# Four engine orders of a gated cross-attention kernel, laid out anew

## The chip, the cores and the metric

One NeuronCore of a Trainium2 chip runs the whole program. The metric is the device time of one execution in microseconds (us), the median of three. The core has five engines that this text names by their labels in the profile: PE (TensorE, matrix multiply; PEld is its weight load), DVE (VectorE), ACT (ScalarE), POOL (GpSimd) and SP, which here only issues DMAs.

## What is computed

Four sequences (b = 0 to 3) of 512 tokens with 128 features pass four residual blocks. A context of 77 rows of 96 features goes with each sequence.

```python
# block 1: attention with a kept top 32 of 77, FiLM, long convolution (S4D), FFN
scores = jnp.einsum('bthd,bghd->bhtg', Q, K) / np.sqrt(DH)        # 4 heads
topv, topi = jax.lax.top_k(scores, 32); probs = jax.nn.softmax(topv, -1)
attn_mean = scatter(probs).mean(heads); c_t = attn_mean @ V
x = layernorm(x_text) * (1 + mod_gate * scale_in) + mod_gate * shift_in
y = irfft(rfft(x) * rfft(K_s4d)) + x * D_skip
xt = x_text + y * (1 + mod_gate * scale_out) + mod_gate * shift_out
xt = xt + gelu(layernorm(xt) @ W1 + b1) @ W2 + b2                 # then a layernorm
# block 2: FFN whose two 512x512 maps are butterfly products
# block 3: attention with 16 heads over the same context
# block 4: eight experts, the best two weighted by a softmax
x = x + jnp.tanh(g) * block(_layernorm(x))                        # around each block
```

## The kernel before, in words

The sequence b is the unit of work, and a tile t = 0 to 3 is 128 of its tokens. All work is cut into named steps such as `film_in/2`, where the number after the slash is b and a digit at the end of the name is a tile, a half or a stage. The dictionary `ORDER` writes out, for each of PE, ACT, DVE and POOL, the order in which that engine takes its steps. Each engine runs its list strictly in order and waits on semaphores for what a step needs. So whatever stands behind a waiting step waits too. No planner runs at build time.

The steps of one sequence are, in order of dependence:

- `score0` to `score3`: PE multiplies, DVE finds the top 32 of 77 for four heads by four rounds of MAX8 and MATCH_REPLACE8 (L1144, L1153), ACT takes the exponentials, POOL picks (`pick`, L1538) and weighs them (`weigh`). In round 1 of a score step DVE adds up what POOL picked for the tile before (`weigh(1)`, L1076), so the DVE stands there until that `pick` is done. `attnT` needs all four `weigh`.
- `film_in`, `dft`, then the spectral product in two halves, `mixr` and `mixi` (seven TENSOR_TENSORs each), `idft`, `film_pre`, `film_out`, `film_add`: FiLM and the long convolution.
- `stat1`, `rs1`, `norm1`, `lift1` (statistics on DVE, root on ACT, scaling on DVE or POOL, transpose on PE), `ffn_up0`, `ffn_up1`, `ffn_down`: the FFN. Then `stat2`, `norm2`, `gain` (POOL), `x1` (the residual sum), `stat3`, `norm3`, `lift3`.
- `fold_up0`, `fold_up1`, `fold_down`: the butterfly block. Then `stat4`, `norm4`, `lift4`.
- `q`, `scoreA0` to `scoreA3` (DVE takes the row maxima), `maxT`, `keyA0` to `keyA2`, `mixA0` to `mixA2`, `normA`, `wo`: attention of 16 heads. Then `stat5`, `lift5`.
- `logits`, `top2`, `units0` to `units3`, `gate0`, `gate1` (POOL), `turn0`, `turn1`, `moe_out`: the experts and the store.

Steps that begin with `s_` are set-up, done once: the convolution's kernel (`s_kgen0`, `s_qarg`, `s_parg`, `s_pexp`, `s_coef`, `s_qal`, `s_pc`, `s_qc`, `s_kern0` to `s_kern3`, `s_freq`), the butterflies made dense (`s_ufly`, `s_udense`, `s_dfly`, `s_dhigh`, `s_dlow` on POOL, `s_t1`, `s_wup`, `s_bup`, `s_t2`, `s_wdn` on PE) and centred or masked weights (`s_m0`, `s_vw`, `s_w1`, `s_cw1`, `s_cwup`, `s_moe`, `s_v1`).

Three other things follow from `ORDER`. The eight PSUM banks are dealt out in the order of PE's list (`place_banks`, first freed, first given), and PE waits for the readers of a bank's former tile. ACT loads a function table whenever the next step needs another set (L782); for a step that leads with a function it does so before it waits. And `made()` finds which engine does a norm, an `x1` or a mix, so these can move from one list to another.

```python
for step, b in SCHEDULE["pe"]:        # likewise "act", "dve", "pool"
    ...
need = table_of.get(func, table[0])
if need != table[0]:                  # an ACT_TABLE_LOAD
```

## Time and profile before

| what | us |
|---|---|
| median of three executions | 362.0 (360.42 to 362.31) |
| the profiled execution | 359.27 |
| its span, first to last instruction | 357.4 |
| PE busy | 269.9 |
| DVE busy | 283.1 |
| ACT busy | 217.0 |
| POOL busy | 195.2 |

The span is 1.9 us shorter than the execution's own time, and that execution is 2.7 us below the median. A busy share is an average over stretches with different limits: until about 226 us DVE works through the sixteen score steps, and from about 162 us to the end PE has the most work. Which of the two is late must be read stretch by stretch. PEclk is the TensorE clock that the chip granted, where 1.0 is 2.4 GHz.

### The profile page before, as it was taken

The page shows a single profiled execution, that of the slowest core. Times are in us where ns is not written, and L with a number is a line of the kernel's source. Part 1 is how long each engine was busy: PE and PEld are TensorE (multiplying, and loading weights), DVE is VectorE, ACT ScalarE, POOL GpSimd, SP SyncE. Part 2 cuts the span into 40 slices and gives each one's busy share as a digit, 9 for nine tenths or more (in the row PEclk, how much of TensorE's full clock was granted, in tenths as well). Part 3 has the DMA queues.
Part 4 walks back from the last instruction along what each step waited for, and adds up shares of the span by engine and source line. Part 5 has one row for each costly group of instructions (what it writes and reads, how often), then busy time and mean ns, then how long its engine had stood idle before and what let it go on. Part 6 is the DMA issues. An engine that isn't in the chain of part 4 may idle for free.

```text
span 357.4 us, 6314 instructions
## 1 busy us (share of the span) xinstructions
PE 269.9 (76%) x1858; PEld 176.5 (49%) x1858; DVE 283.1 (79%) x1402; ACT 217.0 (61%) x472; POOL 195.2 (55%) x271
## 2 busy tenths in 40 slices
...
GB/s 245 383 373 49 1 1 0 1 0 4 3 1 3 0 2 2 1 0 0 3 0 3 0 1 2 0 3 0 2 1 3 0 3 0 2 29 2 0 32 60
DMA packets 6713, 10.82 MB, mean 30 GB/s; under 512 B 660, under 2 KB 4884, under 8 KB 6422
## 3 DMA queue, kind: packets, MB, share of 16 engines
...
q8 instruction: 15, 0.25, 0.3%
...
## 4 chain that ended last, share of the span: by engine, by line
PE 43%; DVE 30%; POOL 16%; issue 3%; DMA 3%; ACT 2%; SPq 1%; POOLq 0%; ACTq 0%; DVEq 0%
PE bank L446 40%; DVE R L1153 8%; DVE V L1144 5%; DMA X<-in_x 3%; DVE MT L1047 2%; POOL arena L1428 2%; POOL bt L1428 2%; POOL k0bd L1428 2%; POOL MT L1428 2%; DVE arena L1047 2%; PE bank L468 2%; POOL sel L1538 1%; DVE st L1093 1%; POOL sel L1428 1%; POOL HN L1485 1%
## 5 line engine op out<-in xcount | busy, mean ns | idle before, releaser
L782 ACT ACT_TABLE_LOAD x37 | 47.5, 1283 | 4.3 <-DMA pack_kgen<-in_kgen 3.7
L1153 DVE MATCH_REPLACE8 R<-V,R 128x77 f32<-128x77 f32 x192 | 40.4, 220 | 0.0
L509 PE MATMUL bank<-pack_first,ASUM 128*77 128x128 f32 x16 | 2.9, 314 | 48.7 <-POOL ASUM L1428 48.7
L788 ACT ACTIVATE arena<-bank 128x512 f32<-128x512 f32 (+2 forms) x67 | 34.8, 598 | 8.1 <-PE bank L446 5.3
L446 PE MATMUL bank<-arena,pack_dft 128*128 128x256 f32 x128 | 34.0, 426 | 5.9 <-DVE arena L1047 4.7
L446 PEld LDWEIGHTS bank<-arena,pack_dft 128*128 128x128 f32 x128 | 27.0, 215 | 13.4 <-DVE arena L1047 6.0
L1428 POOL TENSOR_TENSOR pack_bfly<-pack_bfly,bt 128x512 f32<-128x512 f32 x8 | 8.3, 1049 | 44.8 <-DVE pack_bfly L1047 30.2
L788 ACT ACTIVATE E<-bank,negm,rs 128x77 f32<-128x77 f32 x64 | 21.3, 416 | 18.3 <-DVE negm L1052 18.3
L788 ACT ACTIVATE rs<-mv,cst 128x4 f32<-128x4 f32 x28 | 7.9, 295 | 40.3 <-DVE mv L1096 40.2
L1144 DVE MAX8 V<-R 128x8 f32<-128x77 f32 x192 | 31.1, 222 | 0.0
L509 PEld LDWEIGHTS bank<-pack_first,ASUM 128*77 128x77 f32 x16 | 2.2, 170 | 49.8 <-POOL ASUM L1428 49.6
L1117 DVE TENSOR_REDUCE bt<-bank 128x4 f32<-128x308 f32 x64 | 25.4, 467 | 1.0 <-PE bank L446 0.9
L1428 POOL TENSOR_TENSOR XG<-XG,pack_rows 128x512 f32<-128x512 f32 x4 | 5.1, 1268 | 35.4 <-DVE XG L1052 26.1
L1538 POOL TENSOR_SCALAR sel<-R 128x308 f32<-128x308 f32 x16 | 16.0, 1001 | 15.0 <-DVE R L1153 8.3
L1428 POOL TENSOR_TENSOR k0bd<-sel,w 128x308 f32<-128x308 f32 x16 | 13.3, 829 | 16.9 <-DVE w L1051 16.8
L1047 DVE TENSOR_TENSOR X<-bank,X 128x512 f32<-128x512 f32 x12 | 8.1, 685 | 17.3 <-PE bank L446 17.3
L446 PE MATMUL bank<-pack_bfly,arena 32*128 32x512 f32 (+3 forms) x136 | 21.0, 558 | 0.0
L446 PE MATMUL bank<-pack_moe,LO 128*128 128x512 f32 (+1 forms) x64 | 19.6, 429 | 1.4 <-ACT arena L788 0.7
L1047 DVE TENSOR_TENSOR pack_bfly<-bank,pack_bfly 128x256 f32<-128x256 f32 (+1 forms) x20 | 9.1, 470 | 13.3 <-ACT pack_bfly L788 13.3
L788 ACT ACTIVATE LO<-bank 128x512 f32<-128x512 f32 x16 | 9.4, 596 | 13.8 <-PE bank L468 13.7
L1485 POOL TENSOR_SCALAR HN<-X,rs 128x128 f32<-128x128 f32 x24 | 14.2, 607 | 6.6 <-ACT rs L788 6.6
L788 ACT ACTIVATE arena<-MT 128x128 f32<-128x128 f32 x74 | 17.3, 430 | 0.0
(226 smaller groups left out, 809.1 us busy)
## 6 DMA issues: line engine op xcount, KB each, us to landing
...
```

The source lines that it names most:

```text
L446: return nc.tensor.matmul(out, lhsT, rhs, start=start, stop=stop, **kw)
L468: last = nc.tensor.transpose(o[:, P * t:P * t + P], src[:, b, t, :], I)
L509: last = nc.tensor.transpose(o[0:SK, P * t:P * t + P], ASUM[:, b % 2, t, :], I)
L782: nc.scalar.add_instruction(mybir.InstLoadActFuncSet(name=nc.get_next_instruction_name(), act_func_set_id=need, ins=[], outs=[]))
L788: return nc.scalar.activation(out, in_, func, **kw)
L1047: return nc.vector.tensor_tensor(out, x, y, op)
L1117: nc.vector.tensor_reduce(mx1[:, b % 2, tile, r, :], bank(f"sA{tile}_{r}", b)[:, 0:FLAT] .rearrange("p (h k) -> p h k", h=HG), AX.X, ALU.max)\
L1144: nc.vector.max(V8[:, g % 2, h, r, :], src).then_inc(s["topk_step"], 1)
L1153: nc.vector.match_replace(R8[:, g % 2, r % 2, h, :], V8[:, g % 2, h, r, :], src, NEG)\
L1428: return nc.gpsimd.tensor_tensor(out, x, y, op)
L1485: last = nc.gpsimd.tensor_scalar(dst[:, b, t, :], src[:, b, t, :], rs[:, tile, b, t:t + 1], None, ALU.mult)
L1538: chain(nc.gpsimd.tensor_scalar(sel[:, g % 2, :, :], R8[:, g % 2, 1, :, :], -1.0e38, None, ALU.is_le))
```

## The change

Only `ORDER` changes; every step issues the instructions that it issued before. Four steps go to DVE: `x1/0`, `norm3/2`, `norm4/2` and `norm3/3`. Two go to POOL: `x1/1` and `norm3/1`. The halves of the spectral product stay on their engines (`mixr` on DVE but for b = 3, `mixi` on POOL but for b = 3) and change their places. All four lists are in a new order. The banks follow PE's list, and the number of table loads on ACT follows its list: 37 in the old one, 31 in the new one. The diff is cut where a list goes on.

```diff
--- before.py
+++ after.py
 ORDER = {
     "pe": """
-        s_k0 s_m0 score0/0 s_vw score1/0 s_w1 score2/0 score3/0 score0/1 score1/1 attnT/0 vw/0 s_cw1 s_kern0 s_kern1
-        film_in/0 s_kern2 s_kern3 vw/1 score2/1 s_t1 film_pre/0 score3/1 dft/0 s_freq s_wup score0/2 score1/2 s_cwup
-        s_bup idft/0 vw/2 s_t2 lift1/0 ffn_up0/0 attnT/1 score2/2 ffn_up1/0 s_wdn k1/0 ffn_down/0 film_in/1 vw/3
-        film_pre/1 film_out/0 score3/2 dft/1 score0/3 lift3/0 k1/1 fold_up0/0 fold_up1/0 idft/1 fold_down/0 s_moe
-        film_out/1 s_v1 k1/2 lift4/0 score1/3 attnT/2 lift1/1 q/0 ffn_up0/1 ffn_up1/1 scoreA0/0 scoreA1/0 scoreA2/0
-        film_in/2 scoreA3/0 ffn_down/1 dft/2 film_pre/2 maxT/0 keyA0/0 keyA1/0 score2/3 lift3/1 mixA0/0 fold_up0/1
-        idft/2 film_out/2 fold_up1/1 fold_down/1 keyA2/0 lift1/2 score3/3 mixA1/0 mixA2/0 lift4/1 ffn_up0/2
-        ffn_up1/2 ffn_down/2 q/1 normA/0 k1/3 attnT/3 scoreA0/1 film_in/3 scoreA1/1 film_pre/3 scoreA2/1 wo/0
-        scoreA3/1 dft/3 lift5/0 lift3/2 maxT/1 keyA0/1 keyA1/1 fold_up0/2 units0/0 logits/0 units1/0 idft/3
-        fold_up1/2 units2/0 fold_down/2 units3/0 keyA2/1 mixA0/1 mixA1/1 film_out/3 lift4/2 lift1/3 normA/1 mixA2/1
...
+        s_k0 s_m0 score0/0 score1/0 s_t1 s_vw score2/0 score3/0 score0/1 s_kern0 s_kern1 s_kern2 score1/1 s_kern3
+        score2/1 s_freq s_bup attnT/0 vw/0 s_w1 s_wup s_moe film_in/0 score3/1 dft/0 vw/1 s_t2 film_pre/0 vw/2
+        score0/2 k1/0 idft/0 score1/2 s_cwup attnT/1 film_out/0 s_cw1 film_in/1 score2/2 film_pre/1 lift1/0 dft/1
+        ffn_up0/0 ffn_up1/0 ffn_down/0 vw/3 idft/1 film_out/1 score3/2 s_wdn lift3/0 score0/3 k1/1 fold_up0/0
+        fold_up1/0 fold_down/0 lift1/1 score1/3 ffn_up0/1 ffn_up1/1 ffn_down/1 attnT/2 lift4/0 k1/2 film_in/2 q/0
+        s_v1 scoreA0/0 scoreA1/0 scoreA2/0 scoreA3/0 film_pre/2 score2/3 dft/2 maxT/0 lift3/1 keyA0/0 fold_up0/1
+        fold_up1/1 keyA1/0 fold_down/1 idft/2 keyA2/0 mixA0/0 mixA1/0 film_out/2 score3/3 lift4/1 lift1/2 mixA2/0
+        ffn_up0/2 q/1 ffn_up1/2 scoreA0/1 ffn_down/2 scoreA1/1 attnT/3 normA/0 wo/0 film_in/3 film_pre/3 scoreA2/1
+        scoreA3/1 lift5/0 dft/3 units0/0 units1/0 maxT/1 units2/0 lift3/2 keyA0/1 fold_up0/2 fold_up1/2 mixA0/1
+        keyA1/1 k1/3 fold_down/2 idft/3 keyA2/1 mixA1/1 lift4/2 logits/0 film_out/3 q/2 lift1/3 units3/0 mixA2/1
...
     "act": """
-        s_kgen0 s_cols s_qlag s_plag rs0/0 s_trig rs0/1 s_m0 s_pexp score0/0 s_psin0 norm0/0 s_qsin s_psin1 score1/0
-        s_vw s_qexp score2/0 rs0/2 score3/0 score0/1 vw/0 attnT/0 s_cw1 score1/1 s_kern1 s_kern3 vw/1 s_t1
-        film_pre/0 score2/1 dft/0 s_freq s_wup score3/1 rs1/0 score0/2 s_cwup lift1/0 s_t2 score1/2 vw/2 ffn_up0/0
-        attnT/1 ffn_up1/0 score2/2 k1/0 norm0/1 rs2/0 s_wdn film_pre/1 vw/3 rs3/0 dft/1 rs0/3 score3/2 lift3/0
-        fold_up0/0 score0/3 fold_up1/0 k1/1 rs1/1 rs4/0 s_moe lift4/0 lift1/1 k1/2 attnT/2 q/0 score1/3 ffn_up0/1
-        ffn_up1/1 norm0/2 rs2/1 dft/2 film_pre/2 maxT/0 rs3/1 keyA0/0 lift3/1 keyA1/0 norm0/3 score2/3 fold_up0/1
...
+        s_cols s_kgen0 s_qlag s_plag s_pexp rs0/0 s_trig s_m0 s_psin0 s_psin1 s_qsin score0/0 s_t1 score1/0 rs0/1
+        score2/0 s_vw s_qexp score3/0 s_kern1 s_kern3 score0/1 norm0/0 score1/1 attnT/0 score2/1 s_freq vw/0 s_wup
+        rs0/2 s_moe dft/0 norm0/1 s_t2 film_pre/0 score3/1 vw/1 score0/2 attnT/1 score1/2 vw/2 s_cwup k1/0 rs0/3
+        rs1/0 s_cw1 film_pre/1 lift1/0 dft/1 score2/2 ffn_up0/0 ffn_up1/0 rs2/0 vw/3 s_wdn rs3/0 norm0/2 score3/2
+        rs1/1 lift3/0 fold_up0/0 fold_up1/0 k1/1 score0/3 lift1/1 rs4/0 ffn_up0/1 ffn_up1/1 score1/3 attnT/2 k1/2
+        lift4/0 rs2/1 q/0 film_pre/2 rs3/1 dft/2 maxT/0 score2/3 lift3/1 keyA0/0 fold_up0/1 fold_up1/1 keyA1/0 rs4/1
...
     "dve": """
-        s_kgen0 s_consts s_wq stat0/0 s_qarg s_masks s_k0 stat0/1 s_parg0 nmr0/0 s_parg1 score0/0 s_coef s_edge
-        s_pc0 score1/0 s_pc1 s_pc2 s_pc3 score2/0 stat0/2 s_w1 score3/0 score0/1 weigh3/0 s_qc score1/1 s_kern1
-        film_in/0 s_kern3 score2/1 score3/1 mixr/0 score0/2 film_out/0 nmr0/1 film_add/0 s_bup stat1/0 weigh3/1
-        norm1/0 score1/2 score2/2 ffn_down/0 stat2/0 nmr0/2 norm2/0 film_in/1 stat0/3 stat3/0 score3/2 mixr/1
-        score0/3 film_out/1 weigh3/2 film_add/1 fold_down/0 stat1/1 stat4/0 s_v1 norm1/1 score1/3 scoreA0/0
-        scoreA1/0 scoreA2/0 film_in/2 s_misc scoreA3/0 ffn_down/1 stat2/1 norm2/1 maxT/0 x1/1 stat3/1 norm3/1 nmr0/3
-        mixr/2 score2/3 film_out/2 film_add/2 stat1/2 norm1/2 fold_down/1 stat4/1 score3/3 weigh3/3 ffn_down/2
-        normA/0 stat2/2 scoreA0/1 film_in/3 norm2/2 scoreA1/1 scoreA2/1 stat3/2 wo/0 scoreA3/1 maxT/1 mixi/3 stat5/0
-        film_out/3 units0/0 top2/0 film_add/3 units1/0 fold_down/2 units2/0 stat1/3 stat4/2 units3/0 norm1/3 normA/1
-        wo/1 scoreA0/2 scoreA1/2 stat5/1 scoreA2/2 scoreA3/2 units0/1 maxT/2 ffn_down/3 stat2/3 norm2/3 x1/3 stat3/3
-        top2/1 normA/2 fold_down/3 stat4/3 norm4/3 wo/2 units1/1 moe_out/0 stat5/2 units2/1 units3/1 scoreA0/3
-        scoreA1/3 scoreA2/3 scoreA3/3 units0/2 maxT/3 units1/2 units2/2 units3/2 top2/2 normA/3 wo/3 moe_out/1
...
+        s_kgen0 stat0/0 s_qarg s_wq s_edge s_parg0 s_consts s_k0 s_parg1 s_masks nmr0/0 s_coef s_pc0 s_pc1 score0/0
+        score1/0 s_pc2 s_pc3 stat0/1 score2/0 stat0/2 s_qc stat0/3 score3/0 s_kern1 s_kern3 score0/1 weigh3/0
+        score1/1 s_bup nmr0/1 score2/1 film_in/0 s_w1 nmr0/2 score3/1 mixr/0 score0/2 film_out/0 weigh3/1 score1/2
+        film_add/0 stat1/0 film_in/1 norm1/0 score2/2 mixr/1 ffn_down/0 stat2/0 norm2/0 film_out/1 film_add/1 x1/0
+        stat3/0 stat1/1 score3/2 norm1/1 score0/3 fold_down/0 stat4/0 weigh3/2 score1/3 ffn_down/1 stat2/1 film_in/2
+        norm2/1 s_v1 scoreA0/0 scoreA1/0 scoreA2/0 scoreA3/0 nmr0/3 stat3/1 maxT/0 score2/3 mixr/2 fold_down/1
+        stat4/1 film_out/2 film_add/2 stat1/2 norm1/2 score3/3 scoreA0/1 weigh3/3 s_misc normA/0 ffn_down/2
+        scoreA1/1 wo/0 stat2/2 film_in/3 norm2/2 scoreA2/1 stat5/0 stat3/2 scoreA3/1 maxT/1 norm3/2 units0/0
+        units1/0 units2/0 mixi/3 fold_down/2 stat4/2 norm4/2 film_out/3 film_add/3 stat1/3 norm1/3 top2/0 units3/0
+        scoreA0/2 normA/1 scoreA1/2 scoreA2/2 scoreA3/2 maxT/2 ffn_down/3 stat2/3 wo/1 norm2/3 x1/3 stat5/1 stat3/3
+        norm3/3 normA/2 top2/1 fold_down/3 stat4/3 wo/2 norm4/3 stat5/2 units0/1 units1/1 moe_out/0 units2/1
+        scoreA0/3 units3/1 scoreA1/3 scoreA2/3 scoreA3/3 maxT/3 units0/2 units1/2 units2/2 top2/2 units3/2 normA/3
...
     "pool": """
-        s_row s_ufly pick0/0 s_coef weigh0/0 pick1/0 s_qal weigh1/0 pick2/0 s_udense s_film pick3/0 weigh2/0
-        weigh3/0 pick0/1 s_dfly pick1/1 weigh0/1 pick2/1 film_pre/0 mixi/0 weigh1/1 s_dhigh pick3/1 weigh2/1 pick0/2
-        weigh3/1 s_dlow pick1/2 s_rows k1/0 weigh0/2 weigh1/2 x_bias/0 gain/0 x1/0 pick2/2 norm3/0 mixi/1 film_pre/1
-        weigh2/2 pick3/2 s_v1 weigh3/2 pick0/3 norm4/0 x_bias/1 pick1/3 weigh0/3 gain/1 mixi/2 film_pre/2 weigh1/3
-        k1/1 pick2/3 k1/2 x_bias/2 norm4/1 weigh2/3 pick3/3 weigh3/3 x_bias/3 gain/2 x1/2 film_pre/3 norm3/2 mixr/3
-        k1/3 norm4/2 gate0/0 gate1/0 gain/3 norm3/3 gate0/1 gate1/1 gate0/2 gate1/2 gate0/3 gate1/3
+        s_row s_ufly s_coef pick0/0 s_udense weigh0/0 pick1/0 s_qal s_film pick2/0 weigh1/0 s_dfly pick3/0 weigh2/0
+        pick0/1 weigh3/0 pick1/1 weigh0/1 s_dhigh pick2/1 mixi/0 weigh1/1 s_dlow film_pre/0 pick3/1 weigh2/1 pick0/2
+        weigh3/1 s_rows x_bias/0 pick1/2 film_pre/1 weigh0/2 s_v1 mixi/1 pick2/2 gain/0 norm3/0 weigh1/2 x_bias/1
+        k1/0 k1/1 pick3/2 weigh2/2 pick0/3 weigh3/2 norm4/0 gain/1 pick1/3 x1/1 film_pre/2 norm3/1 mixi/2 norm4/1
+        weigh0/3 pick2/3 x_bias/2 weigh1/3 k1/2 weigh2/3 pick3/3 weigh3/3 gain/2 x1/2 film_pre/3 mixr/3 k1/3 gate0/0
+        gate1/0 gain/3 x_bias/3 gate0/1 gate1/1 gate0/2 gate1/2 gate0/3 gate1/3
```

In the parts left out, PE's new list goes on after `keyA0/0` with `fold_up0/1 fold_up1/1 keyA1/0 fold_down/1 idft/2 keyA2/0 mixA0/0 mixA1/0 film_out/2 score3/3 lift4/1 lift1/2`, and much later with `dft/3 units0/0 units1/0 maxT/1 units2/0 lift3/2 keyA0/1 fold_up0/2 fold_up1/2 mixA0/1 keyA1/1 k1/3 fold_down/2 idft/3`. ACT's new list goes on after `lift1/0` with `dft/1 score2/2 ffn_up0/0 ffn_up1/0 rs2/0 vw/3 s_wdn rs3/0 norm0/2 score3/2 rs1/1 lift3/0`.

## Rows read from the trace of the kernel before

**Rows 1.** Page part 1: busy us, share of the span, instructions.

```profile
PE 269.9 (76%) x1858; PEld 176.5 (49%) x1858; DVE 283.1 (79%) x1402; ACT 217.0 (61%) x472; POOL 195.2 (55%) x271
```

**Rows 2.** Windows, each engine's busy us (x instructions), clock granted to PE, DMA.

```profile
29.00:77.50 48.50, 0.00 (x0) 0.00 (x0) 46.74 (x258) 23.17 (x55) 45.12 (x67) 0.53 0.00 1
95.40:110.90 15.50, 14.79 (x96) 11.60 (x95) 15.36 (x82) 3.71 (x8) 11.95 (x12) 0.99 0.00 1
85.70:162.40 76.70, 67.30 (x472) 51.32 (x472) 74.81 (x437) 39.72 (x91) 61.54 (x81) 0.91 0.01 1
162.40:232.20 69.80, 65.26 (x411) 42.65 (x410) 58.94 (x282) 42.97 (x90) 34.01 (x45) 0.98 0.00 1
232.20:288.85 56.65, 54.66 (x374) 35.57 (x373) 40.34 (x137) 40.29 (x67) 20.39 (x22) 1.00 0.00 1
288.85:354.00 65.15, 61.79 (x420) 34.36 (x416) 32.17 (x150) 41.92 (x77) 9.83 (x11) 0.97 0.04 13
```

**Rows 3.** Page part 5, costliest groups: count, busy, mean ns, idle before.

```profile
L782 ACT ACT_TABLE_LOAD x37 | 47.5, 1283 | 4.3 <-DMA pack_kgen<-in_kgen 3.7
...
L509 PE MATMUL bank<-pack_first,ASUM 128*77 128x128 f32 x16 | 2.9, 314 | 48.7 <-POOL ASUM L1428 48.7
```

**Rows 4.** Timeline of ACT, the start: start us, us, line, op, out<-in, [idle before].

```profile
3.65 1.28 ACT L782 ACT_TABLE_LOAD   x1 [3.65 <-DMA pack_kgen<-in_kgen]
...
5.95 1.28 ACT L782 ACT_TABLE_LOAD   x1
```

**Rows 5.** Timeline of DVE, the first score steps.

```profile
18.03 0.87 DVE L1093 BATCH_NORM_STATS2 st<-X 128x6 f32<-128x128 f32 x4 [1.75 <-DMA X<-in_x]
...
24.19 0.68 DVE L1144 MAX8 V<-bank 128x8 f32<-128x77 f32 x4
...
30.28 0.35 DVE L1047 TENSOR_TENSOR MT<-MT,AO 128x128 f32<-128x128 f32 x1
...
40.49 0.45 DVE L1076 TENSOR_REDUCE sm<-sel 128x4 f32<-128x308 f32 x1
```

**Rows 6.** Timeline of POOL, picks and butterflies.

```profile
31.71 1.00 POOL L1538 TENSOR_SCALAR sel<-R 128x308 f32<-128x308 f32 x1
...
33.58 5.04 POOL L1428 TENSOR_TENSOR MT<-MT 128x128 f32<-128x128 f32 x7
...
44.56 0.46 POOL L1428 TENSOR_TENSOR AO<-AO,MT 128x128 f32<-128x128 f32 x1
...
68.21 0.98 POOL L1538 TENSOR_SCALAR sel<-R 128x308 f32<-128x308 f32 x1
...
79.45 0.65 POOL L1428 TENSOR_TENSOR bt<-pack_bfly 128x64 f32<-128x64 f32 x2
...
91.18 0.46 POOL L1428 TENSOR_TENSOR v<-bt 128x128 f32<-128x128 f32 x1
```

**Rows 7.** Timeline of PE, three steps of the stream.

```profile
156.96 5.41 PE L446 MATMUL bank<-arena,pack_dft 128*128 128x256 f32 x16 [3.84 <-DVE arena L1047]
...
232.22 0.60 PE L509 MATMUL bank<-pack_first,ASUM 128*77 128x128 f32 x4
...
254.34 3.72 PE L446 MATMUL bank<-arena,pack_dft 128*128 128x256 f32 x16 [1.22 <-POOL arena L1428]
```

**Rows 8.** Timeline of POOL, a norm of b = 0.

```profile
143.97 2.35 POOL L1485 TENSOR_SCALAR HN<-X,rs 128x128 f32<-128x128 f32 x4
```

**Rows 9.** Timeline of DVE, half a product twice, and a norm.

```profile
149.62 2.19 DVE L1047 TENSOR_TENSOR MT<-arena,pack_film 128x512 f32<-128x512 f32 x2
...
203.08 1.28 DVE L1047 TENSOR_TENSOR MT<-arena,pack_film 128x512 f32<-128x512 f32 x2
...
312.90 0.87 DVE L1051 TENSOR_SCALAR HN<-X,rs 128x128 f32<-128x128 f32 x4 [0.60 <-ACT rs L788]
```

**Rows 10.** Timeline of ACT, a table load between two activations.

```profile
125.85 1.28 ACT L782 ACT_TABLE_LOAD   x1
127.15 1.27 ACT L788 ACTIVATE arena<-bank,b1f 128x512 f32<-128x512 f32 x2
```

26 lines of the change are left out of this document (13 added, 13 removed).

## The prediction, made before the changed kernel was run

> **What bounds the kernel now.** I read three things in turn: the page's busy times, windows over the stretches, and the timelines of the engines around each moved step. The page gives DVE 283 us and PE 270 us of 357 [rows 1]: no engine has slack to speak of, and neither is full. The windows say where each one rules. Between 29 and 77.5 us PE has nothing, at a granted clock of 0.53, near its lower level of 1.2 GHz, while DVE is busy for 46.7 of 48.5 us [rows 2]. The groups name PE's wait: 48.7 us for POOL's sum of the attention weights, which releases attnT/0 [rows 3]. After film_in/0 leaves PE at 85.7 us, PE is busy for 67.3 of 76.7, 65.3 of 69.8, 54.7 of 56.7 and 61.8 of 65.2 us [rows 2]. Added up, that is 249.0 us of work and 19.3 us of idle time, and PE's last matmul ends at 85.7 + 249.0 + 19.3 = 354.0. DVE is busy for 74.8 of 76.7 us until 162.4 and 58.9 of 69.8 after it [rows 2]. So DVE decides how fast the first half comes and PE how fast the rest goes. I make the sum on PE: the time at which film_in/0 leaves it, its work after that, and its idle time after that.
>
> **PE's work after film_in/0.** Eight steps are now ahead of it that were behind: s_kern2, s_kern3, s_freq, s_wup, s_bup, s_t1, s_moe and score2/1. s_cw1 goes the other way. s_freq, s_wup and s_bup fill most of the window from 95.4 to 110.9, with 14.8 us of PE work [rows 2], less two score steps and s_cwup, some 2.2 us, which gives 12.6. The other five are about 4.1 us and s_cw1 is 1.8. Sum: 12.6 + 4.1 - 1.8 = 14.9, so 249.0 becomes 234.1 us. If the 48.5 us of idle before had no other cost, this would be the gain.
>
> **When film_in/0 leaves PE.** I follow DVE through its new list with the durations of the old trace.
> - ACT now takes s_cols before s_kgen0. It waits for its small input, loads a table (1.28 us), runs a tanh, loads again, and only then makes the first exponential; before, one load stood in front of that [rows 4]. I put the delay at 1.7 us (bounds 0.5 and 2.5). It is paid back: the first score no longer has the 1.75 us wait for the X of b = 1 ahead of it [rows 5].
> - DVE does s_edge, s_coef, s_pc0 and s_pc1 before score0/0, so that step starts at 33.6 instead of 24.2 us [rows 5]. These are no new work, and cost nothing by themselves.
> - POOL takes s_coef before pick0/0. s_coef ran from 33.6 to 45.0, 11.4 us, and pick0/0 ran ahead of it, from 31.7 [rows 6]. Now s_coef starts at 31.7 and pick0/0 is done at about 45.0. The sum of score1/0 needs it; before, that sum ran without a wait, 2.3 us into its step [rows 5]. It would come at 42.2, so DVE stands for 2.8 us, and with it score2/0 and all behind it. Bounds 0 and 4.
> - s_qc stands before score3/0 and needs POOL's s_qal, which ends at about 62: 0.8 us (0 to 3). Two old stalls in score steps, 1.8 us together, fall in with it.
> - POOL takes s_dfly before pick3/0. s_dfly ran from 79.5 to 91.6, 12.2 us, and pick3/0 at 68.2 [rows 6]. Now pick3/0, and weigh3/0 behind it, wait for it, and attnT/0 comes at about 90 instead of 77.6. Its queue (vw/0, s_w1, s_wup, s_moe, film_in/0) follows, but DVE has score1/1 and score2/1 to do meanwhile, so most of this is hidden; less than 1 us is not.
>
> DVE so reaches film_in/0 at about 101 us and film_in/0 leaves PE at 101.2, 15.5 later than before. It reaches mixr/0 at 110.5 instead of 104.9. The 14.9 us that PE saved are spent, and the balance is +0.6 us.
>
> **PE's idle time after that.** Before: 9.4, 4.5, 2.0 and 3.4 us in the four windows [rows 2].
> - To the end of idft/1. mixr/1 now stands before score3/2 and not after it, so the wait of 3.84 us ahead of idft/1 [rows 7] shrinks to about 1. New ones come: attnT/1 is not ready (3), film_in/1 waits for the copy of vw/2 (1.5), which ACT does only after score1/2. I get 7.8, and idft/1 ends at 154 with 189 us of work left, against 162.4 with 182.
> - From there to attnT/3. lift3/0 now follows idft/1 on PE with only score3/2 and s_wdn between. Its chain from the end of mixr/1 at 149.4 is ffn_down/0, stat2/0, a root, norm2/0, film_out/1, film_add/1, x1/0, stat3/0, a root and a norm on POOL of 2.35 us [rows 8]: to 160.4, where PE is free at 156. That is 4.5 us, and fold_up0/0 adds 1.6, because ACT has norm0/2 and score3/2 before the copy of lift3/0. Then s_v1 and scoreA0/0 to scoreA3/0 stand together, paced by DVE, with film_pre/2 and dft/2 behind them: 2.5. The rest is about 1. I get 9.7 where 4.5 was, and attnT/3 at about 238.5 instead of 232.2 [rows 7].
> - From attnT/3 to the end. The work is the same, 115 us. Norms 3/2, 4/2 and 3/3 on DVE take 0.87 us each where POOL needed 2.35 [rows 8, 9], and the wait of 1.22 ahead of idft/3 [rows 7] has more work before it. ACT's single tables and the later idft/3 take some of it. I get 4.9 where 5.4 was.
>
> Idle: 7.8 + 9.7 + 4.9 = 22.4, +3.1 us. The end of PE: 101.2 + 234.1 + 22.4 = 357.7, against 354.0, so +3.7. The last sum and store stay at 3.4. The profiled execution, 359.3 with a span of 357.4, would be 363.0. It lies 2.7 us under the median of 362.0, and I add the same difference to the median: 365.7.
>
> **Two prices that could be other.** mixr/1 on DVE beside mixi/1 on POOL has its first two products in 2.19 us; mixr/2, alone, in 1.28 [rows 9]. So 2 to 3 us hang on each pair. The Trainium skill, page "SBUF — State Buffer", section "Who interferes with whom", says that a DVE instruction with two SBUF inputs and a GpSimd instruction that reads SBUF block each other for a whole instruction. By it mixr/2 and maxT/0, which now meet mixi/2 only in part, could move by that much either way; the rows show the same and the sum stays.
>
> A table load is 1283 ns [rows 3], and the next activation begins 0.02 us behind it [rows 10]. Six fewer are 7.7 us of ACT, which is idle for 140 us in all [rows 1], so I count nothing. The Trainium skill, page "ScalarE: Activation LUTs", section "What ACT_TABLE_LOAD costs", gives 2.66 us with a drain. By that price six switches would be an estimated 16 us; the trace does not show the drain.
>
> **The rivals.**
> - *The early PE work pays.* PE had 48.5 us free, and 14.9 us less work stands behind film_in/0. If POOL's s_coef does not stop DVE, film_in/0 leaves at 98.4, and if the new waits at lift3/0 and scoreA close while the three old ones go (3.84, 1.22 and the norm's 0.6), idle is 13.6: 98.4 + 234.1 + 13.6 = 346.1, -7.9, a median near 354. It decides where PE finds work ready at each step after 154 us. For it: the shorter norms and the earlier mixr/1. Against it: the chain to lift3/0, whose steps stand in this order in two lists. Chance 0.25.
> - *ACT sets the end.* The score steps and the FFNs wait for ACT's loads; six fewer give -7.7, a median of 354.3. Against it: ACT's idle share. Chance 0.05.
> - *It cancels.* The stalls grow by no more than 1 us: within 1.8 us of 362. Chance 0.18.
> - *Forecast*, +3.7 us, 365.7 (364 to 369). Chance 0.35.
> - *Late twice.* DVE reaches score3/3 only when PE has got through mixA0/0 and mixA1/0, which now stand ahead of it, and the delay passes from PE to DVE and back; dft/3, mixr/3 and idft/3 then go behind ten more steps. Idle 29: 101.2 + 234.1 + 29 = 364.3, +10.3, a median near 372. Chance 0.17.
>
> **Range and chances.** The bounds of the terms are about 5 us to each side of the forecast. The range of 8 in 10 takes in the faster rivals at 354, with 1 us below, and the last one at 372: 353 to 372. A change under 0.5%, or 1.8 us, can't be told from none in this kernel. Faster 0.30, the same 0.18, slower 0.52. The slower cases alone run from 364 to 372.
>
> **What would show it.** A wait of about 2.8 us of DVE in score1/0 for POOL's pick, with s_coef ahead of it; attnT/0 near 90 us; film_in/0 leaving PE near 101; mixr/0 near 110; a wait of PE of 4 to 6 us ahead of lift3/0 near 156; attnT/3 after 236. If attnT/3 comes before 230, or PE's idle time after film_in/0 is under 18 us, the forecast is wrong. If DVE does not stop in score1/0, the step that failed is the POOL order.

## The result, and the profile after

The changed kernel takes 367.9 us (median, 367.6 to 371.1) where the kernel before takes 362.1 in the same session. The ratio is 1.019, with a 95% interval of 1.012 to 1.025: slower by 5.7 us. The forecast was 365.7, slower, in a range of 353 to 372. The profiled execution takes 368.1 us, with a span of 366.3; the sum had made 363.0 of it. The executions of some kernels below fall on two levels, up to 9 us apart with nothing changed between them, so a ratio takes only those within 1.5% of the kernel's fastest, and the median of all stands beside it.

The page of the changed kernel, parts 1 and 2 (busy us, share of the span, instructions; then the clock granted to PE in 40 slices, in tenths):

```profile
PE 285.5 (78%) x1858; PEld 186.0 (51%) x1858; DVE 284.6 (78%) x1410; ACT 209.1 (57%) x466; POOL 190.3 (52%) x263
...
PEclk9999996558599958996997889999999999997899
```

The same 1858 matmuls are there as in [rows 1], but PE's busy time is 285.5 us and not 269.9. 15.6 us more for the same work is time at the lower granted clock, or a sequence in which the matmuls overlap less; the page does not part the two. The clock row shows where to look (a slice is 9.2 us): it is low in slices 7 to 11, 15, 16, 19, 22 to 24, 37 and 38.

The windows that answer to [rows 2], from the point where film_in/0 leaves PE (105.9 us) to PE's last matmul (362.2). Columns: length, then busy us (x instructions) of PE, PEld, DVE, ACT and POOL, granted clock, DMA:

```profile
105.90:362.20 256.30, 238.86 (x1437) 153.30 (x1436) 195.39 (x936) 154.75 (x300) 109.78 (x131) 0.93 0.01 4
105.90:158.60 52.70, 43.40 (x218) 33.01 (x218) 50.11 (x255) 23.64 (x54) 40.07 (x48) 0.90 0.01 1
158.60:243.10 84.50, 78.63 (x447) 51.71 (x446) 72.10 (x388) 52.67 (x105) 46.51 (x63) 0.90 0.00 1
243.10:293.10 50.00, 49.96 (x342) 31.89 (x339) 37.83 (x131) 32.09 (x57) 14.46 (x13) 1.00 0.00 1
293.10:362.20 69.10, 66.86 (x439) 36.69 (x436) 35.36 (x163) 46.35 (x84) 8.74 (x8) 0.95 0.04 12
```

256.3 us, of which 238.9 are work and 17.4 idle, where [rows 2] add up to 249.0 of work and 19.3 idle. The clock is 0.90, 0.90, 1.00 and 0.95, where [rows 2] have 0.91, 0.98, 1.00 and 0.97. Between 243.1 and 293.1 us PE is idle for 0.04 us: its queue is full there.

Timelines, in the order of the forecast's checks. DVE at the end of the pick's wait and at film_in/0:

```profile
45.55 0.47 DVE L1076 TENSOR_REDUCE sm<-sel 128x4 f32<-128x308 f32 x1 [4.39 <-POOL sel L1428]
...
105.02 0.69 DVE L1047 TENSOR_TENSOR HN<-bank,HN 128x512 f32<-128x512 f32 x1 [3.74 <-PE bank L446]
```

POOL, the first product of s_coef and the first operation of pick0/0:

```profile
34.03 3.24 POOL L1428 TENSOR_TENSOR MT<-MT 128x128 f32<-128x128 f32 x7
...
43.62 0.98 POOL L1538 TENSOR_SCALAR sel<-R 128x308 f32<-128x308 f32 x1
```

PE: attnT/0, s_wup, film_in/0, attnT/1, lift3/0, attnT/3, idft/3:

```profile
91.92 1.09 PE L509 MATMUL bank<-pack_first,ASUM 128*77 128x128 f32 x4
...
96.07 6.72 PE L446 MATMUL bank<-arena 128*128 128x512 f32 x8
...
103.93 1.95 PE L446 MATMUL bank<-VW,AT 78*128 78x128 f32 x16
...
131.06 1.14 PE L509 MATMUL bank<-pack_first,ASUM 128*77 128x128 f32 x4 [4.77 <-POOL ASUM L1428]
...
165.10 1.11 PE L468 MATMUL bank<-pack_first,HN 128*128 128x128 f32 x4 [4.98 <-POOL HN L1485]
...
243.13 0.66 PE L509 MATMUL bank<-pack_first,ASUM 128*77 128x128 f32 x4
...
269.38 3.62 PE L446 MATMUL bank<-arena,pack_dft 128*128 128x256 f32 x16
```

DVE stands for 4.39 us in score1/0, because pick0/0 begins only at 43.6 behind s_coef. It stands again for 3.74 us at film_in/0, which PE has not finished: s_wup alone takes 6.72 us in its queue. lift3/0 waits 4.98 us for POOL's norm, and idft/3, which waited 1.22 in [rows 7], waits no more.

### The profile page after: what moved, and what is told of

Same layout as the page of the kernel before. It is cut to its first block, busy times and chain, and to the rows that moved or that the text cites. A ratio compares the mean times of both kernels' runs of the same rounds, so it can differ in the third digit from the quotient of the medians.

```text
span 366.3 us, 6304 instructions
## 1 busy us (share of the span) xinstructions
PE 285.5 (78%) x1858; PEld 186.0 (51%) x1858; DVE 284.6 (78%) x1410; ACT 209.1 (57%) x466; POOL 190.3 (52%) x263
## 4 chain that ended last, share of the span: by engine, by line
PE 57%; DVE 18%; POOL 14%; issue 4%; DMA 3%; ACT 1%; SPq 1%; POOLq 0%; ACTq 0%; DVEq 0%
PE bank L446 53%; DVE R L1153 4%; DMA pack_bfly<-in_bfly 3%; DVE arena L1047 3%; DVE V L1144 3%; POOL bt L1428 3%; POOL arena L1428 2%; DVE MT L1047 2%; PE bank L468 2%; POOL MT L1428 2%; POOL AO L1428 1%; DVE KT L1379 1%; POOL bflyl L1428 1%; PE bank L509 1%; POOL k0bd L1428 1%
## 5 line engine op out<-in xcount | busy, mean ns | idle before, releaser
L782 ACT ACT_TABLE_LOAD x31 | 39.8, 1283 | 4.4 <-DMA pack_small<-in_small 3.8
L446 PE MATMUL bank<-pack_bfly,arena 32*128 32x512 f32 (+3 forms) x136 | 23.2, 563 | 16.6 <-POOL arena L1428 15.8
L446 PE MATMUL bank<-arena,pack_dft 128*128 128x256 f32 x128 | 30.2, 390 | 2.3 <-DVE arena L1047 2.1
L446 PE MATMUL bank<-arena 128*32 128x16 f32 (+3 forms) x304 | 15.4, 241 | 17.0 <-issue 17.0
L446 PEld LDWEIGHTS bank<-arena,pack_dft 128*128 128x128 f32 x128 | 24.6, 197 | 7.3 <-DVE arena L1047 3.1
L446 PEld LDWEIGHTS bank<-pack_bfly,arena 32*128 32x128 f32 (+2 forms) x136 | 9.9, 182 | 24.9 <-POOL arena L1428 16.7
L446 PEld LDWEIGHTS bank<-arena 128*32 128x32 f32 (+1 forms) x304 | 10.9, 165 | 21.5 <-issue 21.5
L446 PEld LDWEIGHTS bank<-VW,AT 78*128 78x128 f32 x128 | 18.4, 229 | 3.3 <-issue 2.7
L446 PE MATMUL bank<-VW,AT 78*128 78x128 f32 x128 | 19.3, 316 | 0.8 <-ACT VW L788 0.8
L446 PE MATMUL bank<-M,LO 128*128 128x308 f32 x32 | 15.6, 579 | 4.0 <-DVE maskrow L1276 2.8
L446 PE MATMUL bank<-LO,pack_dft 128*128 128x512 f32 x32 | 17.7, 705 | 0.0
## 6 DMA issues: line engine op xcount, KB each, us to landing
pack_bfly<-in_bfly SPq DMA_DIRECT2D x1, 2420.0 KB, 11.9
pack_dft<-in_dft SPq DMA_DIRECT2D x1, 1536.0 KB, 15.7
```

The source lines that it names most:

```text
L446: return nc.tensor.matmul(out, lhsT, rhs, start=start, stop=stop, **kw)
L782: nc.scalar.add_instruction(mybir.InstLoadActFuncSet(name=nc.get_next_instruction_name(), act_func_set_id=need, ins=[], outs=[]))
```

## The experiments

Twelve kernels were run, in four sessions. Each ratio is to the kernel before as it ran in the same session, on the same chip. Its median was 362.1 us beside the changed kernel, 362.7 beside e2 to e4, 361.8 beside e5 to e8, 360.2 beside e9 to e12 and 362.9 beside e13, so between sessions ratios compare better than medians. Idle time and all steps are read from one profiled execution of each kernel.

| Run | us, median (range) | Ratio to before, 95% | PE's idle us after 106 |
|---|---|---|---|
| changed kernel | 367.9 (367.6 to 371.1) | 1.019 (1.012 to 1.025) | 17.4 |
| e2: changed to 106 us, then before | 374.9 (371.4 to 376.7) | 1.038 (1.032 to 1.044) | 28.0 |
| e8: changed to 160 us, then before | 381.9 (380.8 to 382.4) | 1.057 (1.053 to 1.060) | 29.5 |
| e7: before to 160 us, then changed | 361.5 (359.7 to 363.7) | 1.001 (0.998 to 1.004) | 20.2 |
| e9: before to 170 us, then changed | 356.1 (354.5 to 357.5) | 0.988 (0.981 to 0.994) | 15.4 |
| e6: before to 60 us, then changed | 371.2 (362.7 to 372.8) | 1.002 for its fastest | 15.7 |
| e10: before, changed engines only | 364.8 (360.4 to 369.1) | 1.004 (0.998 to 1.009) | 20.5 |

### Which part of the order costs

A seam kernel takes, on each engine, the steps that the first kernel had started by the time named, in its order, and then all other steps in the order of the second. Nothing else is edited. Four runs of this kind split the change in two. (e1, before's order to 106 us with the changed one behind it, which e2's text names as its mirror, has no time: its lists wait on each other in a circle.)

```diff
 PE, seam of e2 (the changed order above it)
         s_moe film_in/0 score3/1
-        dft/0 vw/1 s_t2 film_pre/0 vw/2 score0/2 k1/0 idft/0 ...
+        s_cw1 vw/1 film_pre/0 dft/0 score0/2 score1/2 s_cwup idft/0 ...
```

> The mirror of e1: the changed order for what the changed kernel had started by 106 us of its trace, the order of before for all others. My theory (set-up): slower than before by 4 to 8 us, ratio 1.012 to 1.022. Rival T (order behind 106 us): ratio 0.998 to 1.005. If both come out slow or both near one, the two parts interact and neither is the cause alone.

Measured: 1.038, more than both theories said. The front of the changed order is bad for before's tail, worse than for its own.

```diff
 PE, seam of e8 (the changed order above it)
         film_out/1 score3/2 s_wdn
-        lift3/0 score0/3 k1/1 fold_up0/0 fold_up1/0 fold_down/0 ...
+        score0/3 lift3/0 k1/1 fold_up0/0 fold_up1/0 fold_down/0 s_v1 ...
```

> The mirror of e7: the changed order to 160 us of its trace, then that of before. Theory F: ratio 1.015 to 1.025, as the changed kernel. Rival T: 1.000 to 1.008. e2, with the seam at 106 us, gave 1.038, more than either kernel: if e8 is also above 1.025, the two orders only fit their own other half, and the seam itself costs.

Measured: 1.057, over both ranges. The halves do not exchange freely. The windows of e2 and e8 from 106 us to PE's last matmul (columns as above) show the cost as idle time of PE:

```profile
106.00:366.10 260.10, 232.14 (x1434) 150.31 (x1432) 192.92 (x922) 158.47 (x303) 112.00 (x137) 0.95 0.01 4
```

```profile
106.00:375.40 269.40, 239.87 (x1437) 154.10 (x1434) 193.64 (x928) 158.92 (x303) 114.19 (x138) 0.92 0.01 4
```

Idle is 260.1 - 232.1 = 28.0 and 269.4 - 239.9 = 29.5 us, where before has 18.8. My reading is that before's tail counts on POOL and DVE being further on than the changed front leaves them; the waits were not followed one by one.

```diff
 PE, seam of e7 (before's order above it)
         fold_up0/0 fold_up1/0 idft/1
-        fold_down/0 s_moe film_out/1 s_v1 k1/2 lift4/0 score1/3 ...
+        s_moe film_out/1 fold_down/0 lift1/1 score1/3 ffn_up0/1 ...
```

> The order of before for what it had started by 160 us of its trace, the changed order for the rest, with the changed engines for those norms and sums that fall behind 160 us (x1/1, norm3/1, norm3/2, norm4/2, norm3/3). Theory F (the loss is made in the front part and carried on): the time of before within 0.5%, ratio 0.995 to 1.005. Rival T (behind 160 us the changed order is worse by itself: 203.6 us for 1228 matmuls against 195.4 us for 1213): ratio 1.010 to 1.020.

Measured: 1.001, inside theory F's range. With the front of before, the changed order behind 160 us costs nothing, though the seam itself leaves PE waiting twice for long between 148 and 172 us, 5.5 us for DVE and 6.7 us for ACT.

```diff
 PE, seam of e9 (before's order above it)
         s_moe film_out/1 s_v1
-        k1/2 lift4/0 score1/3 attnT/2 lift1/1 q/0 ...
+        lift1/1 score1/3 ffn_up0/1 ffn_up1/1 ffn_down/1 attnT/2 ...
```

> The order of before for what it had started by 170 us of its trace, the changed order behind it. Theory L (the end is PE's work, plus its idle time, plus what the lower granted clock adds): behind 185 us the changed order leaves PE 3.0 us idle (0.8, 0.0 and 2.2) where that of before leaves 9.1 (4.1, 2.5 and 2.5), and at 170 us before's PE queue is dense, unlike at 160 (e7: 12 us idle at 150 to 170). So 3 to 6 us faster than before: 356 to 359 us, ratio 0.985 to 0.993. Rival S (every seam costs, as in e2, e7 and e8): 362 us or more.

Measured: 0.988, or 4.1 us under before's 360.2, and the profiled execution 3.7 us under before's. Theory L held, and this kernel beats both. Windows from 106 us to PE's last matmul, of before and of e9:

```profile
106.00:354.00 248.00, 229.22 (x1430) 148.21 (x1430) 186.85 (x884) 154.48 (x297) 109.85 (x135) 0.96 0.01 4
```

```profile
106.00:350.30 244.30, 228.95 (x1430) 148.20 (x1430) 185.15 (x889) 153.34 (x295) 106.95 (x128) 0.97 0.02 4
184.33:212.84 28.51, 27.08 (x171) 18.60 (x170) 24.47 (x104) 16.53 (x32) 16.11 (x16) 1.00 0.00 1
```

Both have 1430 matmuls left, and their work is the same, 229.2 and 229.0 us. The idle time fell from 18.8 to 15.4 us: the whole gain. One wait that went is this one of before, maxT/0 for DVE, whose copies ran beside POOL's mixi/2:

```profile
198.30 0.40 PE L446 MATMUL bank<-pack_att,pack_bfly 128*128 128x128 bf16 x4 [3.71 <-DVE pack_bfly L1047]
```

So the two halves of the change have opposite signs. Its order behind 170 us is worth about 4 us. PE ends 362.2 - 350.3 = 11.9 us later in the changed kernel than in e9, but that is not all the price of the order ahead of 170 us. attnT/2 starts only 0.8 us later (185.08 against 184.33). Up to the end of fold_down/1 the changed kernel has the 24 matmuls of s_v1 more to do, 31.4 us at full clock (e5, below) against 28.5, so 2.9 us. The other 5.0 and 3.2 us are the same matmuls at a lower clock (see "The granted clock"). Lag and work left over are 3.7 us in these two profiles, as much as the tail gains, and 8.2 us are dips of the clock. Whether the front brings the dips on is not shown.

### The front: three repairs that moved a wait

```diff
 POOL
-        s_row s_ufly s_coef pick0/0 s_udense ...
+        s_row s_ufly pick0/0 s_coef s_udense ...
```

> The changed kernel with one step of POOL moved: pick0/0 ahead of s_coef. It takes away the 4.39 us wait of DVE inside score1/0. Theory D (DVE's waits ahead of film_in/0 count): DVE is 4.4 us earlier, up to -4 us on 367.9. Rival P (POOL's chain counts): pick0/0 needs score0/0's last MATCH_REPLACE8 at 39.0 us, so POOL idles from 33.95 to 39.0 and s_coef, s_udense, s_t1, s_film and s_dfly all leave some 5 us later; s_qc on DVE then waits for s_coef (50.5 us, no wait) but s_t1 on PE and s_film move by 5 us: 0 to +5 us. I expect P with a small net: +0 to +3 us against the changed kernel.

Measured: 374.2 us, 1.031 (1.023 to 1.038), where the changed kernel has 1.019: rival P, and more. PE and DVE in e3:

```profile
53.88 2.09 PE L446 MATMUL bank<-pack_bfly,arena 128*128 128x129 f32 x8 [23.60 <-POOL arena L1428]
...
58.32 0.68 DVE L1144 MAX8 V<-bank 128x8 f32<-128x77 f32 x4 [8.29 <-PE bank L446]
```

The wait in score1/0 is gone. But s_udense comes later, PE's s_t1 waits for it, and score2/0 stands behind s_t1 on PE: DVE now waits 8.29 us there.

```diff
 PE
-        score2/1 s_freq s_bup attnT/0 vw/0 s_w1 s_wup s_moe film_in/0 score3/1 dft/0 ...
+        score2/1 s_freq s_bup attnT/0 vw/0 s_w1 s_moe film_in/0 score3/1 s_wup dft/0 ...
```

> The changed kernel with one step of PE moved: s_wup (6.72 us at the lower granted clock) from ahead of film_in/0 to behind score3/1. My theory (the queue on PE ahead of film_in/0 is what the sum mis-sized): film_in/0 leaves PE at 99 instead of 105.9, DVE's wait of 3.74 us there is gone, and the end comes 3.5 to 4 us earlier: 364 us, ratio to before about 1.007. Rival (what DVE gains is lost at the next waits, attnT/1 for POOL's weigh3/1 at 131.0 and lift3/0 for norm3/0 at 165.1): under 1 us gained.

Measured: 370.7 us, 1.017 (1.006 to 1.027). DVE starts on film_in/0 at 100.6 and not at 105.0, and then stands here, for a root that ACT takes only after the copy of s_wup:

```profile
109.18 0.97 DVE L1055 SCALAR_TENSOR_TENSOR nmr<-rs,mv 128x8 f32<-128x8 f32 x1 [5.66 <-ACT rs L788]
```

```diff
 PE as in e4, and on ACT
-        ... vw/0 s_wup rs0/2 s_moe dft/0 ...
+        ... vw/0 rs0/2 s_moe s_wup dft/0 ...
```

> The changed kernel with s_wup behind score3/1 on PE, as in e4, and now also on ACT behind s_moe, so that ACT's rs0/2 (for which DVE waited 5.66 us in e4) doesn't stand behind it. My theory (DVE's work done by 121 us sets the end: in e4 every interval behind 120 us had the length it had in the changed kernel, 3.1 us later): DVE meets film_in/0 at 100.6 and ends mixr/0 near 118 instead of 121.0, and the end is 3 us earlier than the changed kernel's: 365 us, ratio 1.008. Rival (PE's own queue sets it): no gain, 368 us.

Measured: median 369.3, with three of ten executions at 362.7 to 362.9; ratio 1.006 (1.001 to 1.011). ACT's wait went, POOL's took its place. DVE's waits for picks, and POOL's s_dhigh and pick2/1 behind it:

```profile
DVE sm L1076 <- POOL sel L1428: 12.1, 2, 8.7
...
108.52 4.07 POOL L1428 TENSOR_TENSOR arena<-v,pack_bfly 128x512 f32<-128x512 f32 x4 [11.45 <-PE bank L446]
112.55 0.98 POOL L1538 TENSOR_SCALAR sel<-R 128x308 f32<-128x308 f32 x1
```

s_dhigh can start only when PE is through s_wup, and pick2/1, which DVE's score3/1 needs, is queued behind s_dhigh: 8.7 us for DVE. mixr/0 ends at 124.6, not at 118 as I expected and not at 121.0 as in the changed kernel. The profiled execution still took 362.8 us. It lost less in the tail to the clock, as shown below.

The last of these takes before's start, which also puts pick0/0 ahead of s_coef and score0/0 at 24.2 us:

```diff
 PE, seam of e6 (before's order above it)
         score3/0 score0/1 score1/1
-        attnT/0 vw/0 s_cw1 s_kern0 s_kern1 film_in/0 s_kern2 s_kern3 ...
+        s_t1 s_kern0 s_kern1 s_kern2 s_kern3 score2/1 s_freq s_bup attnT/0 ...
```

> What before had started by 60 us of its trace stands first, in its order (pick0/0 ahead of s_coef, DVE's s_kgen0 s_consts s_wq stat0/0 start, score0/0 at 24.2); all the rest in the changed order. Theory D (DVE's lag): at film_in/0 before's DVE is some 7 us ahead of the changed kernel's; score0/0 8.8 us earlier and no wait of 4.4 us in score1/0 are taken over, but s_t1, s_kern0 and s_freq come on POOL behind s_coef and s_film as in before: film_in/0 on DVE 3 to 6 us earlier than 105.0, end 362 to 365 us, ratio 1.000 to 1.008. Rival T (the tail's waits set the time): no change, 368 us, ratio 1.018.

Measured: median 371.2, four executions, one of them at 362.7. DVE has before's lead at 60 us (score1/0 ends at 44.9, without a wait) and has lost it by film_in/0, which it starts at 107.4 after 3.5 us of waiting: s_freq, s_bup, s_wup and s_moe stand ahead of film_in/0 on PE in this order too, and attnT/0 comes at 97.2. Theory D's step fell here: DVE's lead at 60 us does not reach film_in/0, because of what stands ahead of that on PE and POOL. The one execution at 362.7 us is inside its range, but it was not the profiled one.

### The engines alone

```diff
 DVE
-        ... stat0/3 stat3/0 ... maxT/0 x1/1 stat3/1 norm3/1 ... maxT/1 mixi/3 ...
+        ... stat0/3 x1/0 stat3/0 ... maxT/0 stat3/1 ... maxT/1 norm3/2 mixi/3 ...
-        ... stat4/2 units3/0 ... stat3/3
+        ... stat4/2 norm4/2 units3/0 ... stat3/3 norm3/3
 POOL
-        ... gain/0 x1/0 ... gain/1 mixi/2 film_pre/2 ... norm3/2 ... norm4/2 ... norm3/3
+        ... gain/0 ... gain/1 x1/1 film_pre/2 norm3/1 mixi/2 ...
```

> The kernel before with its orders, but x1/0, norm3/2, norm4/2 and norm3/3 on DVE and x1/1 and norm3/1 on POOL, as in the changed kernel. My theory (the engines of these six steps matter little; what costs is the order): ratio 0.995 to 1.005. Rival E (DVE is the bound and gets 2.1 us more of work): ratio 1.006 or more.

Measured: ratio 1.004 (0.998 to 1.009), with three executions of ten at 360.4 to 360.7 and the rest at 364 to 369; the median is 4.6 us over before's. The profiled one, 365.2 us, is of the second kind. From 106 us to the end of PE:

```profile
106.00:359.90 253.90, 233.38 (x1426) 149.53 (x1425) 185.76 (x890) 155.07 (x296) 104.00 (x126) 0.94 0.01 4
```

PE's idle time behind 106 us is 253.9 - 233.4 = 20.5 us, 1.7 more than before's 18.8. Its work takes 4.2 us more for four matmuls fewer, at a clock of 0.94 where before has 0.96. The ratio bears my theory out, and the three fastest executions are within 0.6 us of before's median. But seven of ten lie above every one of the 19 executions of before in that session (358.7 to 363.5). That is hardly chance, and by the median of all, 1.013, rival E would hold. So it is not shown that the engines of the six steps cost nothing; what they cost, if they do, comes with a lower clock on PE more than with waits.

### The granted clock

The changed tail stands in three kernels with the same matmuls between the start of attnT/2 and the end of fold_down/1 (195), and between maxT/3 and the last moe_out/3 (192). The changed kernel, e5 and e7, in that order:

```profile
185.08:221.53 36.45, 35.62 (x195) 24.94 (x194) 29.93 (x123) 17.25 (x34) 15.80 (x16) 0.86 0.00 1
329.75:362.21 32.46, 30.22 (x192) 15.87 (x190) 11.60 (x60) 19.53 (x36) 4.13 (x4) 0.89 0.05 17
```

```profile
186.52:217.96 31.44, 30.83 (x195) 21.67 (x194) 27.79 (x123) 17.07 (x34) 16.14 (x16) 1.00 0.00 1
326.19:357.04 30.85, 28.63 (x192) 15.54 (x190) 11.59 (x60) 19.50 (x36) 4.13 (x4) 0.94 0.06 18
```

```profile
183.85:218.62 34.77, 33.94 (x195) 24.22 (x194) 29.77 (x115) 17.06 (x35) 15.78 (x16) 0.90 0.01 1
326.84:356.06 29.22, 26.98 (x192) 15.39 (x190) 11.60 (x60) 19.50 (x36) 4.13 (x4) 1.00 0.06 19
```

The same 195 matmuls take 36.45 us at a clock of 0.86, 34.77 at 0.90 and 31.44 at 1.00; the same 192 take 32.46 at 0.89, 30.85 at 0.94 and 29.22 at 1.00. So 5.0 and 3.2 us of the changed kernel's time are missing in the best of the three traces, e5 for the first stretch and e7 for the second. Everything between the two stretches has the same length to 0.1 us. PE's queue is full there, so each microsecond lost reaches the end.

Next, PE was kept at work in its waits. Transposes of the identity go into the bank that the waiting step has claimed; nothing reads them.

```diff
+            WARM = {("attnT", 1): 28, ("lift3", 0): 30}
+            NAMES = {"s_kern0": "kern0", "s_freq": "fr0"}
+
+            def warm(step, b):
+                for _ in range(WARM.get((step, b), 0)):
+                    nc.tensor.transpose(bank(NAMES.get(step, step), b)[:, 0:P], I, I)
...
             for step, b in SCHEDULE["pe"]:
+                if (step, b) in WARM:
+                    claim(NAMES.get(step, step), b)
+                    warm(step, b)
```

> The changed kernel with 28 transposes of the identity into attnT/1's bank and 30 into lift3/0's, while PE waits there (4.77 us at 126 us, 4.98 us at 160 us). They compute nothing that is read. Theory C (PE's idle waits bring the lower granted clock, and from 165 us on PE's queue sets the end): the granted clock stays near 1.0 at 164 to 171 us, score0/3, k1/1, fold_up0/0 take 2.3 us less, later dips may move: the end 2 to 6 us earlier, 362 to 366 us. Rival (another resource sets the end there): under 1 us.

Measured: 361.5 us, 359.3 to 363.9 in ten executions, 1.004 (1.000 to 1.008), where the changed kernel has 1.019. film_in/1 in the changed kernel, then the filler and film_in/1 in e11:

```profile
134.67 3.75 PE L446 MATMUL bank<-VW,AT 78*128 78x128 f32 x16 [0.77 <-ACT VW L788]
```

```profile
125.31 3.22 PE L463 MATMUL bank<-pack_first 128*128 128x128 f32 x28
...
131.70 2.74 PE L446 MATMUL bank<-VW,AT 78*128 78x128 f32 x16 [1.61 <-ACT VW L798]
```

Step by step, e11's trace stands 2.5 us ahead of the changed kernel's at attnT/1, 3.75 at lift1/0 behind film_in/1, and 3.6 at the end. Behind the second filler the lead grows to 4.7 us and is back at 3.75 at fold_up0/0. So the filler ahead of attnT/1 gave 1.25 us, and the one ahead of lift3/0 nothing. The first 2.5 us come from the start: POOL's s_ufly begins at 14.95 instead of 17.00, when pack_bfly has landed (9.9 against 11.9 us from its issue), and s_wup took 5.72 instead of 6.72 us. That part is the execution's, not the filler's, and the difference of 1.5% between the ratios, some 5 us, is larger than what this pair of traces explains.

> The changed kernel with 84 transposes of the identity while PE waits for s_kern0's operands (15.3 us at 53 us) and 22 while it waits for s_freq's (4.1 us at 77 us). Theory C: s_freq 7.5 to 4.6 us, s_wup 6.7 to 3.4 us, film_in/0 leaves PE near 99 instead of 105.9 and DVE's wait of 3.74 us there is gone: 3 to 4 us earlier at mixr/0 (118 instead of 121.0) and at the end, 364 us. Rival (the granted clock doesn't follow PE's activity, or the transposes themselves delay s_kern0): 368 us or more.

The edit is `WARM = {("s_kern0", 0): 84, ("s_freq", 0): 22}`. Measured: 368.7 us (363.7 to 369.5), 1.015 (1.003 to 1.026): no gain that can be told. Windows of e12 while PE fills its wait, and around s_wup, then the same windows of e11, which has the same lists and no filler here:

```profile
53.00:68.00 15.00, 8.82 (x114) 8.62 (x116) 14.86 (x75) 6.30 (x24) 14.35 (x15) 0.86 0.00 1
92.00:102.00 10.00, 10.00 (x31) 5.70 (x30) 8.67 (x70) 5.16 (x15) 4.94 (x7) 0.70 0.00 1
```

```profile
53.00:68.00 15.00, 1.30 (x97) 1.33 (x101) 14.86 (x80) 6.18 (x24) 14.42 (x14) 0.54 0.00 0
92.00:102.00 10.00, 10.00 (x30) 5.69 (x29) 7.83 (x64) 4.88 (x15) 4.80 (x7) 0.67 0.00 1
```

and s_wup and film_in/0 in e12:

```profile
94.94 5.20 PE L446 MATMUL bank<-arena 128*128 128x512 f32 x8
...
101.28 1.95 PE L446 MATMUL bank<-VW,AT 78*128 78x128 f32 x16
```

While PE fills its wait the clock is higher, 0.86 against 0.54. Around s_wup there is hardly a difference, 0.70 against 0.67, and s_wup takes 5.20 us where e11 has 5.72. film_in/0 leaves at 103.2 where I had 99, and DVE starts on it at 102.4, as in e11 (102.5). So theory C holds for the wait and fails for s_wup: the clock falls again between the filler and s_wup, at 91.2 us in e12 and 91.9 in e11, with PE at work. The last section shows what stands ahead of that fall.

> e9 (before's order to 170 us, the changed order behind it) with 22 transposes of the identity into idft/1's bank while PE waits there (3.85 us at 153 us) and 14 into attnT/2's (2.72 us at 171.6 us). In e11 the 28 transposes ahead of attnT/1 let film_in/1 run at the full granted clock, 1.95 instead of 3.75 us, and 1.25 us of that stayed to the end; the 30 ahead of lift3/0 gave nothing. Theory C (a filled wait gives back what the steps just behind it lost to the lower clock, if they are on the chain): idft/1 takes 3.7 instead of 5.4 us and the steps behind attnT/2 lose 1 to 2 us less: 1 to 3 us below e9, 353 to 355 us. Rival (the fillers only fill): 356 us, as e9.

The edit is e9 with `WARM = {("idft", 1): 22, ("attnT", 2): 14}` and `NAMES = {"idft": "y"}`. Measured: 359.3 us (356.6 to 366.6), 0.990 (0.986 to 0.994): no better than e9. e9's idft/1 and a wait behind it, and e13's filler with idft/1:

```profile
156.81 5.41 PE L446 MATMUL bank<-arena,pack_dft 128*128 128x256 f32 x16 [3.85 <-DVE arena L1047]
...
174.28 0.66 PE L468 MATMUL bank<-pack_first,HN 128*128 128x128 f32 x4 [2.73 <-DVE HN L1051]
```

```profile
151.94 2.56 PE L463 MATMUL bank<-pack_first 128*128 128x128 f32 x22
155.97 3.72 PE L446 MATMUL bank<-arena,pack_dft 128*128 128x256 f32 x16 [1.47 <-DVE arena L1057]
```

idft/1 took 3.72 instead of 5.41 us, as expected, and the steps behind it came 2.4 us earlier as far as lift1/1; then the wait ahead of lift1/1 cost 1.2 us more of lower clock than in e9. The expectation has two things wrong. film_in/1 took 2.74 us in e11, not 1.95. And the 2.73 us wait at 171.6 is lift1/1's (the row reads HN), not attnT/2's, so my second filler stood where PE did not wait and cost its own 1.5 us. Last, the 171 matmuls from attnT/2 to fold_down/1 took 31.8 us at 0.89, in e13:

```profile
184.68:216.50 31.82, 30.18 (x171) 21.19 (x170) 25.72 (x101) 16.30 (x32) 15.72 (x16) 0.89 0.01 2
```

where e9, in the second row of its windows above, had 28.5 at 1.00. A dip that e9 did not have took back what one fewer had given.

## Why the prediction was right, and where it was not

The direction and the number held: +3.7 forecast, +5.7 measured, and the profiled execution 5.1 us above its sum. The sum itself held less well, term by term:

| Term | Forecast | Measured |
|---|---|---|
| film_in/0 leaves PE | 101.2 | 105.9 |
| PE's work after it | 234.1 | 238.9 |
| PE's idle time after it | 22.4 | 17.4 |
| End of PE | 357.7 | 362.2 |

**film_in/0 leaves PE.** The chain was right. s_kgen0 on DVE ends 1.7 us later, and attnT/0 comes at 91.9, forecast 90. POOL's order stops DVE for 4.4 us where I had 2.8. Most of the difference is DVE's: its sum could have run at 41.2, and I had 42.2. The pick is done at 45.5, forecast 45.0, because s_ufly took 17.0 us and not 15.0, and s_coef 9.6 and not 11.4. DVE reaches film_in/0 at 101.3, forecast 101. The step that was mis-sized is PE's queue ahead of film_in/0, of which the forecast says that "less than 1 us is not" hidden. That fits s_wup as it is in before, first row; in the changed kernel the same eight matmuls take 6.72 us at a clock of 0.53, behind the s_bup of the second row:

```profile
100.58 3.60 PE L446 MATMUL bank<-arena 128*128 128x512 f32 x8
```

```profile
88.42 3.63 PE L446 MATMUL bank<-arena 128*128 128x1 f32 x32
```

DVE so waits 3.74 us and mixr/0 starts at 114.4, not 110.5. It is not a PE that had stood idle: nothing keeps PE waiting from 81.05 us on (last section).

**PE's work.** I carried 249.0 - 14.9 with before's clock in it. Two stretches of the tail ran at 0.86 and 0.89, and e5 and e7 show what the same matmuls cost without that: 5.0 and 3.2 us less. The measured work is 4.8 us over the forecast, since before's 249.0 has dips of its own; how much they are, and whether the 14.9 was exact, was not separated. No term of the sum stood for the clock. That is the largest thing the forecast lacked, and no rival named it.

**PE's idle time.** The waits that I named came, nearly at their sizes: attnT/1 4.77 (3 forecast), film_in/1 0.77 (1.5), idft/1 0.78 (1), lift3/0 4.98 (4.5). But I added 1.6 for fold_up0/0, which is 0.04, 2.5 for the scoreA group, which is none, and 4.9 for the last stretch, which is 2.3. The forecast said that idle time under 18 us would make it wrong, and it is 17.4. So by its own test this part of the mechanism fell: idle time was to grow by 3.1 us and fell by 1.9. The changed tail is better than before's, and e9 shows it alone (15.4 against 18.8 us of idle time, -4 us of time). Which of the moved steps closed the gaps was not separated.

The three errors are +4.7, +4.8 and -5.0 us, and two of them cancel. That the total came within 2 us was in part luck: the slower time was forecast from idle time that shrank, and came in part from a clock that the sum did not have.

**The rivals.** "The early PE work pays" was half right: the tail does close, but lag and left-over work of the front take as much again, and the dips of the clock come on top. "ACT sets the end" has nothing for it: six table loads fewer (31, 39.8 us in all) and ACT 8 us less busy, in a slower kernel. The Trainium skill's 2.66 us a switch, page "ScalarE: Activation LUTs", section "What ACT_TABLE_LOAD costs", is not seen here: the mean of the 31 loads is again 1283 ns, and no row has the drain that the page adds to the load. "Late twice" asked for idle time of 29 us, and it was not there.

**The pair on the shared memory.** The two prices left at zero moved as the rows of before suggested: maxT/0, now alone, takes 1.25 us where it took 5.26 beside mixi/2, and mixr/2, now beside mixi/2, takes 6.86 where it took 3.72. 4.0 us less and 3.1 more. The Trainium skill, page "SBUF — State Buffer", section "Who interferes with whom", has this rule of whole instructions that block each other, and the trace agrees.

What stays open: why the clock falls in the tail in some executions and not in others, and so how much of the measured 5.7 us belongs to the order. Without its two dips the profiled execution would be at an estimated 368.1 - 8.2 = 359.9 us, beside 359.3 for that of before, which has dips of its own. All four executions of the changed kernel took 367.6 us or more, so the dips may well come with its order; no run here tests that.
